# Moving transfers between three DMA queues, and turning one row on TensorE, in a two-layer graph network kernel

## The reference

```python
h = relu(layernorm(x))
mask = adj > 0;  deg = sum(mask, axis=1)
nb = (mask @ h / max(deg, 1)) @ W_nb + b_nb
x1 = x + relu(concat(h @ W_self + b_self, nb) @ W_comb + b_comb)
h1 = relu(layernorm(x1))
Wh = h1 @ W                                  # 4 heads of 64
e[n,h,m] = leaky_relu(sl[n,h] + sr[m,h]), where adj or n == m, else -inf
out = x1 + elu(softmax(e over m) @ Wh)
```

## Time and profile before

| | us |
|---|---|
| median of two runs | 862.31 (861.78 and 862.83) |
| profiled execution, its own time | 865.33 |
| its span | 863.3 |
| PE busy in it | 798.6 |
| aggregation, from the first L581 to the last tile's L970 | 84.8 to 363.4 |
| granted clock of TensorE, mean share of full speed | 0.977 |

### The profile page before, as it was taken

One profiled execution on the slowest core, in us unless ns is written; L12 is line 12 of the kernel. 1 busy time (PEld: TensorE's weight loads), 2 busy tenths in 40 slices (PEclk: granted clock), 3 DMA queues, 4 the chain that ended last, 5 costly groups with the idle time before them and its releaser, 6 DMA issues.

```text
span 863.3 us, 26084 instructions
## 1 busy us (share of the span) xinstructions
PE 798.6 (93%) x10789; PEld 730.2 (85%) x10789; DVE 697.1 (81%) x1339; ACT 563.3 (65%) x839; POOL 177.1 (21%) x255
## 2 busy tenths in 40 slices
PE   5897779996999999879999999999999999999995
PEld 4343668885888888768999999999999999999995
DVE  3898557775677777588898999898999889998884
ACT  3574012221222222388999998999989999989992
POOL 0111356674576675300000000000000000000000
PEclk9999889999999999979999999999999999999998
DMA  8689999999999999330041011311101410111001
GB/s 218 171 255 274 301 307 321 315 307 235 271 243 259 295 273 258 96 90 26 1 97 49 10 39 49 71 34 41 49 8 41 97 49 10 39 49 49 8 17 37
DMA packets 90115, 115.68 MB, mean 134 GB/s; under 512 B 61616, under 2 KB 63472, under 8 KB 90064
## 3 DMA queue, kind: packets, MB, share of 16 engines
q1 hardware_dynamic: 70240, 64.71, 29.1%
q10 hardware_dynamic: 9824, 29.50, 12.1%
q0 software_dynamic: 10000, 20.86, 8.1%
HBM read 98.17 MB, written 16.85 MB: 133 GB/s over the span
## 4 chain that ended last, share of the span: by engine, by line
PE 54%; DVE 16%; ACT 11%; DMA 10%; issue 5%; POOL 3%; DVEq 0%; ACTq 0%; POOLq 0%
PE ps_t L581 9%; PE ps_t L583 9%; ACT stage L762 8%; PE ps_x L633 8%; PE ps_t L633 8%; PE ps_a L633 8%; DMA x_scratch<-late 6%; PE ps_w L633 4%; DMA own_scratch<-mask 4%; PE ps_h L633 4%; DVE stage L1059 4%; POOL rows L464 2%; DVE stage L1049 2%; DVE stage L1070 2%; PE ps_w L602 2%
## 5 line engine op out<-in xcount | busy, mean ns | idle before, releaser
L581 PE MATMUL ps_t<-g,mask 128*128 128x257 f16 x1024 | 234.2, 277 | 3.0 <-DVE mask L957 2.9
L583 PE MATMUL ps_t<-g,mask 128*128 128x256 f16 x1024 | 233.8, 276 | 0.0
L762 ACT ACTIVATE stage<-rows,sr 128x1024 int8<-128x1024 f32 x192 | 204.2, 1170 | 5.7 <-PE ps_w L633 5.7
L762 ACT ACTIVATE stage<-bits,sr 128x1024 int8<-128x1024 f32 x192 | 204.3, 1169 | 2.5 <-PE ps_w L633 2.5
L1059 DVE SCALAR_TENSOR_TENSOR stage<-stage,mask 128x1024 int32<-128x1024 int32 x128 | 156.1, 1220 | 21.8 <-ACT stage L762 21.1
L633 PE MATMUL ps_x<-g,stage 128*128 128x130 f16 x2048 | 158.5, 219 | 10.0 <-DVE stage L1070 4.7
L633 PE MATMUL ps_t<-g,stage 128*128 128x130 f16 x2048 | 158.5, 219 | 0.0
L633 PE MATMUL ps_a<-g,stage 128*128 128x130 f16 x2048 | 158.3, 219 | 0.0
L633 PEld LDWEIGHTS ps_x<-g,stage 128*128 128x128 fp8e4 x2048 | 127.3, 97 | 12.1 <-issue 12.0
L633 PEld LDWEIGHTS ps_t<-g,stage 128*128 128x128 fp8e4 x2048 | 127.3, 97 | 0.2
L633 PEld LDWEIGHTS ps_a<-g,stage 128*128 128x128 fp8e4 x2048 | 127.4, 97 | 0.2
(11 more groups left out here) (132 smaller groups left out, 865.8 us busy)
## 6 DMA issues: line engine op xcount, KB each, us to landing
mask<-in_adj SPq DMA_DIRECT2D x88, 256.0 KB, 11.1
mask<-in_adj ACTq DMA_DIRECT2D x64, 256.0 KB, 17.7
stage<-in_adj SPq DMA_DIRECT2D x58, 256.0 KB, 7.4
stage<-in_adj ACTq DMA_DIRECT2D x46, 256.0 KB, 10.5
own_scratch<-mask POOLq DMA_DIRECT2D x16, 256.0 KB, 5.1
rows<-own_scratch POOLq DMA_DIRECT2D x32, 128.0 KB, 6.7
rows<-in_x POOLq DMA_DIRECT2D x128, 32.0 KB, 7.1
x_scratch<-late POOLq DMA_DIRECT2D x32, 128.0 KB, 9.0
```

Of the source, the lines that this page charges most:

```text
L581: nc.tensor.matmul(ps_t32[e][:, 0:D + 1], at, g[:, 2 * kk + b, D:2 * D + 1], start=kk + b == 0, stop=kk == NK - 1 and b == 1, skip_group_c ...
L583: last = nc.tensor.matmul(ps_t32[e][:, 0:D], at, g[:, 2 * kk + b, 0:D], start=False, stop=kk == NK - 1 and b == 1, skip_group_check=True)
L762: nc.scalar.activation(sign_bytes(sgn, k, b), srow[gr % 2].rearrange("p (r n) -> p r n", n=2 * P), ACT.Sign, bias=sr[:, 2 * k + b, H + gr ...
```

## The change

The diff, with the removal of the function `issued_at` left out. It does four things.

1. In the prologue ACT issues the adjacency: group k/2 - 1 behind `high_hT(k)` for each even k from 2 to 14, so seven groups; SP issues none before its last x block. `BOTH` becomes 7.
2. From group 7 on SP issues all four quarters of each group, in the order 0, 2, 1, 3.
3. The rows are issued by ACT: those of tiles 0 and 1 behind block k = 4 of the prologue, those of t + 2 behind `norm1(t)`. Each waits for the one own store that it reads. POOL is left with the stores of own, Wh and x1, and waits for no landing.
4. At t = 9 PE transposes the 8 columns of `s` in two pieces (`first_s`), ACT copies them into `s0_row`, 4 partitions of 1 KB, and POOL stores that at t = 10.

```diff
@@ sync
             x_rows(sp, 3)
-            adj_rows(sp, 0, range(UN))
             for k in range(XR, NK):
                 sp.wait_ge(h_ready, k - XR + 1)
                 x_rows(sp, k)
-                if k % 3 == 1:
-                    adj_rows(sp, k // 3, range(UN))
-            for n in range(NK // 3, 2 * NT):
-                adj_rows(sp, n, range(UN if n < BOTH else UN // 2))
-
-            sp.wait_ge(s0_out, 32)
+            for n in range(BOTH, 2 * NT):
+                adj_rows(sp, n, (0, 2, 1, 3))
+
+            sp.wait_ge(s0_out, 16)
@@ gpsimd
-            def row(t):
-                e = t % 2
-                pool.dma_start(own[:, e, :], own_d[t // 2, :, e * D:(e + 1) * D]).then_inc(row_in[e], 16)
-                for a in range(UN):
-                    pool.dma_start(xt[a * UP:(a + 1) * UP, e, :], x_v[a, t // 2, :, e * D:(e + 1) * D]
-                                   ).then_inc(row_in[e], 16)
...
-            for k in range(NK - 2):
+            for k in range(NK):
                 store_own(k)
-            for b in range(2):
-                pool.wait_ge(own_out[b], 16 * (NP2 - 1))
-            row(0)
-            row(1)
-            store_own(NK - 2)
-            store_own(NK - 1)
-            for b in range(2):
-                pool.wait_ge(own_out[b], 16 * NP2)
             for t in range(NT):
-                if t + 2 < NT:
-                    pool.wait_ge(x1_ready, t + 1)
-                    row(t + 2)
                 if t:
                     store_wh(t - 1)
                 store_x1(t)
-                if t == NJ + 1:
-                    pool.wait_ge(sr_ready, NJ)
-                    with nc.allow_non_contiguous_dma("s is turned from a column into a row"):
-                        for e in range(2):
-                            pool.dma_start(s0_d.rearrange("o (j p e) -> e p (o j)", p=P, e=2)[e],
-                                           sr[:, 0:NJ, 0:1].rearrange("p (j e) o -> p e (j o)", e=2)[:, e]
-                                           ).then_inc(s0_out, 16)
+                if t == NJ + 2:
+                    pool.wait_ge(s0_ready, 1)
+                    pool.dma_start(s0_d.rearrange("o (j n) -> (o j) n", n=2 * P), s0_row).then_inc(s0_out, 16)
@@ tensor
+            def first_s():
+                pe.wait_ge(sr_ready, NJ)
+                for e in range(2):
+                    last = nc.tensor.transpose(ps_s0[:, e * P:(e + 1) * P],
+                                               sr[:, 0:NJ, 0:1].rearrange("p (j e) o -> p e (j o)", e=2)[:, e],
+                                               ident[:, :])
+                last.then_inc(s0T_ready, 1)
...
+                if t == NJ + 1:
+                    first_s()
@@ scalar
+            def row(t):
+                e = t % 2
+                act.wait_ge(own_out[t // 2 % 2], (t // 4 + 1) * 16)
+                act.dma_start(own[:, e, :], own_d[t // 2, :, e * D:(e + 1) * D]).then_inc(row_in[e], 16)
+                for a in range(UN):
+                    act.dma_start(xt[a * UP:(a + 1) * UP, e, :], x_v[a, t // 2, :, e * D:(e + 1) * D]
+                                   ).then_inc(row_in[e], 16)
...
                 high_hT(k, k % 2)
+                if k % 2 == 0:
+                    adj_rows(act, k // 2 - 1, (0, 2, 1, 3))
+                if k == 4:
+                    row(0)
+                    row(1)
             highs(NK - 2, 0)
             highs(NK - 1, 1)
-            for n in range(BOTH, EARLY + 8):
-                adj_rows(act, n, range(UN // 2, UN))
-
...
                 norm1(t, t % 2)
-                for n in issued_at(2 * t):
-                    adj_rows(act, n, range(UN // 2, UN))
+                act.wait_ge(x1_ready, t + 1)
+                row(t + 2)
                 high_h1T(t, t % 2)
-                for n in issued_at(2 * t + 1):
-                    adj_rows(act, n, range(UN // 2, UN))
                 copy_wh(t, t % 2, t // 2)
+                if t == NJ + 1:
+                    act.wait_ge(s0T_ready, 1)
+                    nc.scalar.activation(s0_row.rearrange("q (n e) -> q e n", e=2),
+                                         ps_s0.rearrange("q (e n) -> q e n", e=2), ACT.Copy).then_inc(s0_ready, 1)
@@ module
-BOTH = 9
+BOTH = NK // 2 - 1
```

More of the change, by code:

```diff
@@ L192, in build @@
         ps_r = ps_x[1]
+        ps_s0 = ps_x[0][0:NJ // 2, 0:2 * P]
+        s0_row = junk[0:NJ // 2, 0:2 * P * 4].bitcast(F32)
         ps_mm = ps_x + ps_a
@@ L247, in build @@
         s0_out = sem("s0_out")
+        s0T_ready = sem("s0T_ready")
+        s0_ready = sem("s0_ready")
         rmax_ready = sem("rmax_ready")
@@ L1305 @@
 SLOT, LAST_IN = raw_slots()
-def issued_at(step):
-    done = EARLY + 8
-    for now in range(step + 1):
-        new = [n for n in range(done, min(done + 2, 2 * NT)) if LAST_IN[n] <= now + 6]
-        if now == 0:
-            new = [n for n in new if n < EARLY + 10]
-        done += len(new)
-    return new
 def reads_early(gr):
```

## The result

The changed kernel took **869.98 us** in the median of two runs (867.72 and 872.23), against 862.31: ratio **1.0109**, 95% interval 1.0079 to 1.0138. Slower, by about 1%; 857.7 had been forecast. Every ratio here is to the kernel before on the same chip, and leaves out executions more than 1.5% above the fastest of the same kernel; ranges and medians of runs have all of them.

A forecast was written before the change was run, and what follows sets the result against it. PE was taken to pace the aggregation at 7.92 us a tile, with ACT lacking room in the prologue. Prologue loss 16.5 less aggregation gain 21.1 gave -4.6 us: 857.7 for the median, range 845 to 870.

The forecast's parts named there:

- Five row issues per tile on ACT: Aggregation: five issues take 2.4 us, making ACT's L733 0.4 us late, hidden by 1.3 us of room before PE.
- fourth rival: Aggregation: row issues dearer than 0.65 us make Wh hold PE; at 0.75 each, 15 us more, 872.7; chance 0.05.
- The prologue: Prologue: issues on ACT delay the next roots and, with clock loss, cost 16.5 us, with ends of 11 and 22.
- The clock term: Prologue: PE's wait of over 6 us behind k = 4 lowers its granted clock, costing 1.4 us.
- The three long tiles: Aggregation: tiles 1, 3 and 13 lose 5.6, 7.4 and 9.1 us to late rows and x1 stores; all would go.
- third rival: Prologue: own stores landing above 7.3 us become the wait; at 9.27, 12 blocks lose 2.0 each, 881.7; chance 0.07.
- second rival: Transfers up to the aggregation's end do not keep up; at 285 GB/s loads end 4.3 us later, 862.0; chance 0.20.
- SP alone: Aggregation: SP issuing all adjacency quarters keeps up, but the last five groups may come late: 0 to 6.0, taken as 1.5 us.

The follow-up runs named there:

- three and two: Changed kernel with three of a tile's five row issues ahead of ACT's copy of transposed h1 and two behind it; ratio 1.0030 to the kernel before.
- rows apart: Kernel before with PE-turned s and POOL waiting only for stores read; tile 0's rows behind POOL's fifth own store, tile 1's behind ninth; 842.31 us, ratio 0.9774.

## Why the prediction was wrong

**The step that failed** is "Five row issues per tile on ACT", put at 0.4 us late and covered by 1.3 us of room. The mechanism stood in the text as the fourth rival, with 0.05. Both sizes in the step were wrong, and it took both.

*The price.* All of x's issues in the changed kernel (ns, least, median and most):

```profile
L678 ACTq DMA_DIRECT2D rows<-in_x x128: 317/592/1683, 39.9 to 355.3; - x128
```

The price of 0.479 was the median of x transfers in the prologue, where it was right (1.86 and 2.09 for four). In the aggregation the median of the 116 issued from 110 to 350 us was 0.598. A run of five took 2.25 to 3.84 us, 2.89 by the median, where the step had 2.4. So L731 started 2.99 us behind L724 by the median, 1.0 us late and not 0.4.

*The room.* The 1.3 us were the distance from the end of L998 to PE's Wh product. But DVE itself has the next tile's L970 behind L998 in its own order, and from L970 hang the next root, the next h1 and its copy. Before, L970 came 1.78 us behind the start of L998, and 0.56 to 0.74 of that was a wait for PE; the idle times of 0.65, 0.78 and 0.60 in the earlier trace rows had shown this. In the changed kernel it comes 0.96 to 1.17 us behind in nearly every tile and waits for PE in none of tiles 1 to 29. So only 0.6 to 0.8 us of room were there, and the median run is above it. Once it is used up, ACT and DVE pass a tile on between them and PE follows: from L970 to L724 3.75 us, to L731 whatever the issues take, to L998 0.41, to the next L970 0.97 or 1.14. At t = 11 that is 3.75 + 3.95 + 0.42 + 0.96 = 9.08, the length of tile 12; with the median run it is 8.2, 0.3 over 7.92. Thirty tiles at 0.3 make some 8 of the 11.1 us, by this estimate. The spread of single issues (up to 1.68 us) made tiles unequal, but it is not the main cost: short runs give some of it back. This reading rests on the rows; no run changed the room alone. With 1.3 us of room a median run would have cost nothing, and with runs of 2.4 us neither.

Against the changed kernel's second execution, which lost 12.4 us in the aggregation, three and two recovered 11.8. The prediction had the earlier trace rows with 3.1 us as the dearest single issue before it, and argued the median of another stretch against it.

**The prologue** was right: +15.4 us for tile 0 (93.72 to 109.08) against 16.5. By the distances of the copies (L683, before L687): behind k = 4 10.73 us instead of 3.46, so 7.3 for 6.7; behind 6, 8, 10 and 12 together 7.1 for 7.6. The clock term came as well: from block 5 to 6, with no issue behind block 5, it was 5.07 instead of 3.46, so 1.6 for 1.4. The granted clock was 0.57 and 0.58 over 44 to 48 and 48 to 52 us, where it had been 1.00 before, and PE had stood 6.65 us ahead of it. Behind k = 14 it was 1.7 for nothing, but behind the last copy 1.8 us came back. Block 2 came 1.6 us earlier than before, which nobody had forecast and no run explains; without that the sum would have been half a microsecond too low instead of 1.1 too high.

The Trainium skill's "DMA: Bandwidth & Descriptors", section "Issuing engines are not separate DMA queues", calls the issuing time "usually small relative to the DMA itself". Against the transfer that holds here too: 0.6 us by the median to issue a row of x, 7.4 from issue to landing. Against the work of the engine that issues it does not: 15 us in the prologue and 11 in the aggregation, while the same tile rows issued by POOL were free. With the other half, that all queues end on the same 16 engines, the trace is consistent: over 94 to 340 us the DMA share was 1.01 before and 1.03 after.

**The three long tiles** went as said: 5.6, 7.4 and 9.1 us, of which only the last was taken out alone (8.6 us in medians). Tile 3 still took 9.14 us in the changed kernel, as its issues held it too.

**Own stores** did not become the wait (1.9 us in two), so the third rival fell. **The supply** (second rival, 0.20) did not stop the changed kernel in its profile: DVE waited for no adjacency there, so "SP alone" cost nothing of its 1.5 us. In the pair where only the queue differs, DVE waited 31.3 us for it in one execution, and the medians lie 9.2 us apart.

**The offset.** The sum was made against an execution 3.0 us over its median and carried over. The changed kernel's profiled one was the shorter of its two. So of the miss of 12.3 us (869.98 less 857.7), the aggregation's mis-sized step is 8.1 (11.1 lost for 3.0), the prologue gives 1.1 back, and the other 5.3 lie between the profiled executions and their medians (3.0 before; 2.3 after).

**The range**, up to 870, held the median of 869.98 by a hair, which is luck; the sign was wrong, because a step with half the room that it was given had one price, too low, and a chance of 0.05 of being dearer.

## What to carry to other kernels

Issues of transfers on a computing engine are instructions with a price of their own, here 0.35 to 0.6 us and now and then 1.7; take it from the stretch where they will stand. Count the whole run of them ahead of an instruction that others wait for, and follow what waits to every engine, in each engine's own order: the room is the shortest of these ways, here DVE's idle time before its next instruction and not PE's. Split or move a run until it ends inside the room (three and two, rows apart): the same transfers then cost nothing, and stretches where an engine seems idle may be full of issues already. Waits for "all stores so far" on a queue were worth more here than the choice of queue: making each wait for what it reads, and turning a column on TensorE rather than scattering it, gave 2.3% with the queues left as they were.

## What the runs showed of the hardware

- Issues of the 32 KB row transfers on ACT took 0.47 and 0.52 us each at k = 4 and 0.598 by the median in the aggregation, with single ones of 1.68; on POOL its median was 0.50 over the whole kernel. Why it varies on ACT was not measured.
- With the DMA engines busy throughout (1.04), the rate still differed between executions and kernels: 281 GB/s with the adjacency over one queue, 331 over two, in the same stretch. The changed kernel itself moved 354 GB/s in one profiled execution and 286 in the other (110 to 180 us), so one queue does not force the lower rate; what chooses stays open.
- TensorE's granted clock was 0.57 over 28.3 to 31.5 us before, with PE busy throughout the stretch and a wait of 3.13 us ahead of it. In the changed kernel it was 0.57 over 24 to 28, behind the same wait of 3.13 us that ended earlier there, 1.00 over 28.3 to 31.5, and 0.57 and 0.58 over 44 to 52, behind a wait of 6.65 us. Behind a wait of 2.9 us before the aggregation's first product it was 1.00 in two executions and 0.57 (102 to 106 us) in three with the same prologue; what decides is not shown.
